# Cross-attention scores as one full-precision matmul, with earlier context and value-weight splits

## The reference

```python
q = (query @ wq).reshape(bs, sq, N_Q_HEADS, D_K).transpose((0, 2, 1, 3))
k = (key @ wk).reshape(bs, sk, N_KV_HEADS, 1, D_K)   # repeated for the 4 query heads of a group
v = (value @ wv).reshape(bs, sk, N_KV_HEADS, 1, D_V)
q = _apply_rope(q, curr_seq_pos)
k = _apply_rope(k, curr_seq_pos)
raw = jnp.einsum('bhqd,bhkd->bhqk', q, k) / scale
attn = jax.nn.softmax(raw + mask, axis=-1)
out = jnp.einsum('bhqk,bhkd->bqhd', attn, v)
```

## Time and profile before

| | |
|---|---|
| time, median of 3 runs | 913.37 us (911.8 to 914.2) |
| the profiled execution | 913.87 us |
| its span, first to last instruction | 911.5 us |
| busy in the span: PE, PEld | 869.6 us (95%), 721.2 us (79%) |
| DVE, ACT, POOL | 654.2 us (72%), 473.1 us (52%), 556.1 us (61%) |
| mean granted clock of TensorE | 0.988 |

### The profile page before, as it was taken

One profiled execution on the slowest core, in us unless ns is written; L12 is line 12 of the kernel. 1 busy time (PEld: TensorE's weight loads), 2 busy tenths in 40 slices (PEclk: granted clock), 3 DMA queues, 4 the chain that ended last, 5 costly groups with the idle time before them and its releaser, 6 DMA issues.

```text
span 911.5 us, 15714 instructions
## 1 busy us (share of the span) xinstructions
PE 869.6 (95%) x4780; PEld 721.2 (79%) x4780; DVE 654.2 (72%) x2171; ACT 473.1 (52%) x1509; POOL 556.1 (61%) x486
## 2 busy tenths in 40 slices
PE   7998899899999799999999999999999998999995
PEld 6787777687777588888888888888888887787884
DVE  5465688778877677777777777777777778546546
ACT  5335777877773355555555555555555556340310
POOL 4625866776677666666666666666666688463002
PEclk9999999999999999999999999999999999999998
DMA  8678999768768011311311313113122123000000
GB/s 284 242 222 190 222 205 177 164 164 171 162 202 300 26 36 38 130 39 36 128 36 45 118 36 127 36 36 128 36 78 85 36 70 105 12 24 24 24 12 35
DMA packets 68370, 96.64 MB, mean 106 GB/s; under 512 B 7232, under 2 KB 44352, under 8 KB 67264
## 3 DMA queue, kind: packets, MB, share of 16 engines
q1 hardware_dynamic: 68288, 95.65, 37.4%
HBM read 68.33 MB, written 27.26 MB: 105 GB/s over the span
## 4 chain that ended last, share of the span: by engine, by line
PE 79%; POOL 6%; DVE 5%; issue 4%; ACT 3%; DMA 1%; SPq 1%; POOLq 0%; ACTq 0%; DVEq 0%
PE banks L35 65%; PE banks L1135 4%; PE banks L1115 3%; PE banks L767 3%; PE banks L785 2%; PE banks L1136 2%; PE banks L758 1%; POOL x L1683 1%; POOL B_wv L171 1%; ACT C_prob L1056 1%; DMA heads_k<-heads_k_d 1%; POOL C_t L1271 1%; POOL B_prob L581 1%; PE banks L122 1%; SPq L213 1%
## 5 line engine op out<-in xcount | busy, mean ns | idle before, releaser
L35 PE MATMUL banks<-C_wo,C_o 128*128 128x512 f32 x768 | 191.8, 399 | 1.9 <-DVE C_o L1232 1.0
L35 PE MATMUL banks<-xT,C_w 128*128 128x512 f32 x768 | 186.6, 392 | 1.1 <-DVE xT L137 0.8
L35 PEld LDWEIGHTS banks<-xT,C_w 128*128 128x128 f32 x768 | 144.3, 189 | 31.9 <-issue 2.0
L35 PEld LDWEIGHTS banks<-C_wo,C_o 128*128 128x128 f32 x768 | 140.5, 190 | 30.6 <-issue 1.9
L1047 ACT ACTIVATE C_q<-C_t 128x512 fp32r<-128x512 f32 x64 | 40.5, 632 | 166.1 <-POOL C_t L1271 166.1
L688 ACT ACTIVATE B_prob<-B_prob,B_top 128x128 f32<-128x128 f32 x256 | 99.5, 391 | 40.1 <-DVE B_top L853 40.0
L1279 POOL TENSOR_TENSOR C_q<-C_t,C_q 128x512 fp32r<-128x512 f32 x64 | 82.8, 1294 | 46.0 <-ACT C_q L1047 46.0
L1056 ACT ACTIVATE C_prob<-C_prob,C_top 128x128 f32<-128x128 f32 x256 | 99.0, 391 | 0.0
L581 POOL TENSOR_TENSOR B_prob<-B_prob,B_rden 128x512 f32<-128x512 f32 x64 | 66.5, 1041 | 36.3 <-DVE B_rden L862 36.2
L1271 POOL TENSOR_TENSOR C_t<-C_t,C_t 128x512 f32<-128x512 f32 x64 | 82.8, 1294 | 6.2 <-DVE C_t L1189 5.9
L171 POOL TENSOR_TENSOR C_w<-stage,C_w 128x512 fp32r<-128x512 f32 x32 | 41.1, 1285 | 54.6 <-ACT C_w L166 54.5
(11 more groups left out here) (147 smaller groups left out, 1918.4 us busy)
## 6 DMA issues: line engine op xcount, KB each, us to landing
C_kv<-cross_kv_d SPq DMA_DIRECT2D x8, 2048.0 KB, 8.5
cross_kv_d<-B_k_out SPq DMA_DIRECT2D x16, 512.0 KB, 3.4
cross_kv_d<-B_v_out SPq DMA_DIRECT2D x16, 512.0 KB, 4.7
stage<-wq_dram SPq DMA_DIRECT2D x32, 256.0 KB, 2.6
stage<-wo_dram SPq DMA_DIRECT2D x32, 256.0 KB, 2.6
heads_q<-heads_q_d SPq DMA_DIRECT2D x96, 64.0 KB, 4.0
heads_k<-heads_k_d SPq DMA_DIRECT2D x96, 64.0 KB, 4.1
heads_q_d<-cT SPq DMA_DIRECT2D x8, 512.0 KB, 2.6
```

Of the source, the lines that this page charges most:

```text
L35: mm = eng.matmul(out, stationary[i], moving[j], start=first and n == 0, stop=last and n == len(PASSES) - 1)
```

## The change

- Cross scores: the rotated keys and queries are kept as plain float32, and scores(n) is one float32 matmul of 128 columns for each head, into bank n % 2; it waits for minima(n - 2). The hi and lo copies of keys and queries go (`key_hi`, `key_lo`, `tile_hi`, `tile_lo`), POOL's sum writes the key or query tile itself, the stored keys take half the bytes, and DVE's L1202 goes. The mask is negated once by ACT.
- Context pieces are loaded behind tiles 7 to 15 and split with tiles 16 to 20.
- The first four value pieces are split ahead of step 0.
- ROW, ROOT and NORMAL stand one step earlier.

```diff
-    PIECES = (("k", 0, -1), ("v", 0, 0), ("v", 1, 0), ("v", 2, 1), ("v", 3, 1), ("o", 0, 3), ("o", 1, 4), ("k", 1, 6),
+    PIECES = (("k", 0, -1), ("v", 0, -1), ("v", 1, -1), ("v", 2, -1), ("v", 3, -1), ("o", 0, 3), ("o", 1, 4), ("k", 1, 6),
-    OT, CLOSE, ROW, ROOT, NORMAL, TURN, TAKE = 13, (14, 15), 16, 17, 18, 19, 20
+    OT, CLOSE, ROW, ROOT, NORMAL, TURN, TAKE = 13, (14, 15), 15, 16, 17, 19, 20
...
+    LOAD_BEHIND = {7: (0,), 9: (1,), 11: (2,), 13: (3, 4), 15: (5, 6, 7)}
+    CONTEXT_AT = (16, 17, 18, 18, 19, 19, 20, 20)
...
-            if i >= self.QK // 2 and i % 2 == 1:
-                self.load_piece(eng, self.CONTEXT + (i - self.QK // 2) // 2)
-        for n in range(self.CONTEXT + C, len(self.pieces)):
-            self.load_piece(eng, n)
+            for n in self.LOAD_BEHIND.get(i, ()):
+                self.load_piece(eng, self.CONTEXT + n)
...
+            wait(eng, self.s_kout[j % 2], 16 * (j // 2))
             t1, t2 = self.t1[j % 2][:, :], self.t2[j % 2][:, :]
-            eng.tensor_tensor(t1, t1, t2, ALU.add).then_inc(self.s_sum, 1)
+            eng.tensor_tensor(self.k_out[j % 2][:, :, :], by_batch(t1), by_batch(t2), ALU.add).then_inc(self.s_sum, 1)
...
+    def negate_mask(self, eng):
+
+        eng.wait_ge(self.s_mask, 16)
+        eng.activation(self.mask[:, :, :], self.mask[:, :, :], ACT.Copy, scale=-1.0).then_inc(self.s_negated, 1)
...
             if n % self.Q == 0:
-                eng.wait_ge(self.s_qlo, n + self.Q)
+                eng.wait_ge(self.s_sum, n + self.Q)
...
-            wait(eng, self.s_top, n)
+            wait(eng, self.s_top, n - 1)
             tok = slice(s % 4 * S, (s % 4 + 1) * S)
-            both = self.kv[g % 2][:, 2 * S * s:2 * S * (s + 1)]
+            keys = self.kv[g % 2][:, S * s:S * (s + 1)].bitcast(F32)
             for h in range(self.Q):
-                out = self.sc[:, h // 2, h % 2, :, :].rearrange("p j s -> p (j s)")
-                q = self.q[s // 4]
-                eng.matmul(out, q[0][:, h, tok], both, start=True, stop=False)
-                mm = eng.matmul(out[:, 0:S], q[1][:, h, tok], both[:, 0:S], start=False, stop=True)
+                mm = eng.matmul(self.sc[n % 2][:, h * S:(h + 1) * S], self.q[s // 4][:, h, tok], keys, start=True, stop=True)
...
-            heads = self.prob[:, n % 2, :].rearrange("p (a h s) -> p a h s", a=2, h=2)
-            for a in range(2):
-                added = eng.tensor_tensor(heads[:, a], self.sc[:, a, :, 1, :],
-                                          self.mask[:, n % B, :].unsqueeze(1).broadcast_to([P, 2, S]), ALU.subtract)
-            added.then_inc(self.s_masked, 1)
-            eng.wait_ge(self.s_masked, n + 1)
             eng.memset(self.carrier[:, :], 0.0)
             for h in range(self.Q):
                 last = eng.tensor_tensor_reduce(
-                    self.prob[:, n % 2, h * S:(h + 1) * S], self.sc[:, h // 2, h % 2, 0, :],
-                    self.prob[:, n % 2, h * S:(h + 1) * S], 1.0, 3.4e38, ALU.add, ALU.min,
-                    self.top[:, n % 2, h:h + 1])
+                    self.prob[:, n % 2, h * S:(h + 1) * S], self.sc[n % 2][:, h * S:(h + 1) * S],
+                    self.mask[:, n % B, :], 1.0, 3.4e38, ALU.add, ALU.min, self.top[:, n % 2, h:h + 1])
```

More of the change, by code:

```diff
@@ L271, in pieces_with @@
         return [self.AHEAD + i] if i < C else [self.VALUES + i - self.Q_DONE] * (0 <= i - self.Q_DONE < C) + \
-            [self.CONTEXT + i - self.QK] * (i >= self.QK)
+            [self.CONTEXT + k for k, tile in enumerate(self.CONTEXT_AT) if tile == i]
     def load_piece(self, eng, n):
@@ L473, in __init__ @@
         self.v_out = pool("v_out", 88, [P, 2, HG, 2, P], F32R)
-        self.k_out = [pool(f"k_out{i}", (96, 132)[i], [P, 4, 2, S], F32R) for i in range(2)]
+        self.k_out = [pool(f"k_out{i}", (96, 132)[i], [P, 4, S]) for i in range(2)]
         self.bout = pool("bout", 126, [P, D])
@@ L542, in sync @@
                 loaded += 1
-            j = self.tile("k", n, 4)
+            j = self.tile("k", n, 2)
             if j is not None:
[L545 to L549, removed]
+                eng.wait_ge(self.s_sum, j + 1)
+                eng.dma_start(self.kv_d[j // 2][:, j % 2 * HALF:(j % 2 + 1) * HALF],
+                              self.k_out[j % 2][:, :, :].rearrange("p b s -> p (b s)")).then_inc(self.s_kout[j % 2], 16)
             j = self.tile("v", n, 2)
@@ L693, in scalar @@
             self.value_hi(eng, j)
-        j = self.tile("k", n, 2)
-        if j is not None:
-            self.key_hi(eng, j)
         self.scalar_pieces(eng, n)
@@ L910, in vector @@
             eng.wait_ge(self.s_pj, self.FILL.index(("k", j)) + 1)
-            wait(eng, self.s_klo, j - 1)
+            wait(eng, self.s_sum, j - 1)
             if j == 1:
@@ L968, in __init__ @@
         self.kv = [pool(f"kv{i}", (36, 16)[i], [P, KV], F32R) for i in range(2)]
-        self.q = [[pool(f"q{half}{lo}", 72 + 16 * half + 8 * lo, [P, self.Q, HALF], F32R) for lo in range(2)]
-                  for half in range(2)]
+        self.q = [pool(f"q{half}", 72 + 8 * half, [P, self.Q, HALF]) for half in range(2)]
         self.prob = pool("prob", 132, [P, 2, D])
@@ L992, in live, with query @@
         return 0 <= n - lag < self.NS
-    def query(self, r, lo):
-        return by_batch(self.q[r // self.Q % 2][lo][:, r % self.Q, :])
+    def query(self, r):
+        return by_batch(self.q[r // self.Q % 2][:, r % self.Q, :])
     def split(self, n):
@@ L1039, in piece_hi @@
         self.ring.hi(eng, self.first + i, self.target(i)[0])
-    def tile_hi(self, eng, r):
-        eng.wait_ge(self.s_sum, r + 1)
-        if r == self.Q:
-            for i in range(2):
-                eng.wait_ge(self.before.s_vout[i], 16 * B)
-        eng.activation(self.query(r, 0), by_batch(self.t1[:, r % 2, :]), ACT.Copy).then_inc(self.s_qhi, 1)
+    def negate_mask(self, eng):
+        eng.wait_ge(self.s_mask, 16)
+        eng.activation(self.mask[:, :, :], self.mask[:, :, :], ACT.Copy, scale=-1.0).then_inc(self.s_negated, 1)
     def exponentials(self, eng, n):
@@ L1185, in rotate @@
         eng.wait_ge(self.s_pj, r + 1)
-        wait(eng, self.s_qlo, r - 1)
+        wait(eng, self.s_sum, r - 1)
         eng.tensor_tensor(by_batch(t1), by_batch(bank), cos, ALU.mult).then_inc(self.s_cos, 1)
@@ L1270, in tile_sum @@
         t1, t2 = self.t1[:, r % 2, :], self.t2[:, r % 2, :]
[L1271 to L1280 removed]
+        eng.tensor_tensor(self.query(r), by_batch(t1), by_batch(t2), ALU.add).then_inc(self.s_sum, 1)
     def gpsimd(self, eng, n):
@@ L1370, in sync @@
             if n == self.DOWN:
-                eng.wait_ge(self.before.s_qlo, self.before.TILES)
+                eng.wait_ge(self.before.s_sum, self.before.TILES)
                 for t, name in ((self.gate, "gate"), (self.gamma, "gamma"), (self.beta, "beta")):
```

56 lines of the change are left out of this document (11 added, 45 removed).

## The result

| | before | after |
|---|---|---|
| median of 4 runs, same chip | 913.79 us (911.8 to 915.87) | 888.68 us (887.6 to 889.99) |
| ratio after / before | | 0.9726, 95% interval 0.9699 to 0.9753 |
| profiled execution, span | 913.87, 911.5 us | 889.44, 887.3 us |
| granted clock over the span | 0.988 | 0.995 |

The account below looks back on a forecast made before the run. It took steady stage C to be bound by PE alone, with PE waits elsewhere; terms -5.4 - 3.1 + 0.5 - 1.1 - 5.5 - 0.9 + 0.6 = -14.9 us gave 898.5 us, range 891 to 907 us.

Parts of the forecast that it names:

- Rows a step forward elsewhere: Stage B, the other six sequences: no such wait to remove, PE's transposes can be slightly late; +0.5 us.
- Steps 0 to 4 of stage C: ACT no longer stalls on query tiles, one division wait and one slow stretch remain; -5.2 us, -5.5 with scores(0).
- More comes back: Rival: remaining idle stretches bring no 1.2 GHz level and score blocks cost the lower bound; 892 to 895 us, 13%.
- Steady steps and end of stage C: Stage C: float32 score blocks cost +0.6 us over 64 steps; removing DVE's L1202 shortens waits at the end, -0.9 us.
- The first rival: Stage C scores dearer, PE's rate set by columns: 1.27 us a block, +20 us, 918 us in all; 8%.
- Start of stage B: Value pieces ready early and heads on time: -3.9 us by step 8, -1.5 for a vanished slow stretch; -5.4 us.
- Steps 32 to 36: Stage B: the root stands ahead of value pieces, the lo half is gone, the fourth value piece is late next; -3.1 us.
- End of stage B: Last division and ACT's copy come earlier without key-tile halves, -1.1 us; scores(0) needs no lo half, -0.3 us.
- After stage C: The rest of the kernel after stage C: no change, 0 us.

Follow-up runs that it names:

- root_first: Kernel before with the row's root ahead of the key tile's lo half in POOL's order, no work removed: 909.37 us, ratio 0.9948.
- pool_load_back: after_rows_back plus one unused 128x512 subtraction on POOL ahead of the root, where the lo half stood: 894.75 us, ratio 0.9789 to the kernel before.
- after_rows_back: Changed kernel with ROW, ROOT and NORMAL put one step later again: 887.65 us, ratio 0.9709 to the kernel before.
- heads_first: Changed kernel with three weight pieces loaded behind the heads of step 12 of stage B instead of ahead: 886.33 us, ratio 0.9719 to the kernel before.
- early_only: Kernel before with only the earlier context loads and splits and the first four value pieces split ahead of step 0: 908.85 us, ratio 0.9946.
- rows_only: Kernel before with only ROW, ROOT and NORMAL one step earlier: 906.49 us, ratio 0.9912.
- scores_only: Changed kernel with the pieces and row steps put back, leaving the full-precision scores and what goes with them: 895.96 us, ratio 0.9798 to the kernel before.
- port_free: Kernel before with POOL made to wait for the row's normalise before its next division: 910.25 us, ratio 0.9971.
- longer_wait: Changed kernel with one more POOL subtraction ahead of the division PE waits for in step 3 of stage C: 890.62 us, ratio 0.9743 to the kernel before.

## Why the prediction was wrong

The sign and most places were right; the size was off by 10 us, and one step failed.

- **Rows a step forward elsewhere, +0.5 us: the failed step.** It said: "In the other six sequences no wait of that kind shows." Five of them had one, 0.86 to 0.95 us each; the row of PE's waits names them in one line, and the timeline of one sequence at steps 32 to 36 was taken for an exception where it was the rule made worse by value pieces. The same step failed a second time in the credits: the 1.27 us of the lo half ahead of the root was counted in steps 32 to 36 only, though POOL's order is the same every eight steps. root_first, pool_load_back and after_rows_back show that this is the cause, and that the row step, which the forecast looked at, adds nothing once the lo half is gone. With the smaller wait at step 46 it makes -2.7 us in each of B 16 to 32 and B 36 to 56, and part of the -2.8 at the end of B: some 7 of the 9.3 us that the forecast's sum lacked. That share is worked out from the waits and the steps of the traces; root_first by itself, with heads and waits moved elsewhere, gave 5 us.
- **Steps 0 to 4 of stage C, -5.2: measured -7.0** from scores(0) to the transposes of step 4, as the forecast counted. The mechanism was right: ACT has no query tile between exponentials, values(1) follows the outputs, one wait for the division is left (2.10 us against my 2.3). The 1.7 us for a slow stretch behind it did not come. That was in part luck: of the five kernels with this same wait of 2.10 us, two (heads_first, pool_load_back) had the stretch, and three had not. The rival "More comes back" named this, the missing stretch at the start of stage B and the cheaper records; all three came, but its 892 to 895 us still lies above 888.68, since it lacked the row waits too.
- **Steady steps and end of stage C, +0.6 - 0.9: measured -1.5.** A record costs 0.112 us and not 0.12. Twenty steps, C 20 to 40, take 149.93 us against 150.40 before, 0.023 a step: 0.023 x 59 = -1.4 us. The -0.9 for the end of C is not there: PE's starts move by 0.2 us from C 59 to 63. The first rival, which scaled the old block of 0.95 us by its columns, would have given +20 us. An estimate says why it fell: if a record streams its 128 columns twice, 8 records want 8 x 256 / 2.4 GHz = 0.85 us, less than the old block's 0.95, which its own 1536 columns (0.64 us) did not fill. What else held the old block up, weight loads as the forecast has it, is argued and not shown.
- **Start of stage B, -5.4: measured -5.4, by two errors that cancel.** At step 8 it was 5.3 us instead of 3.9, because the 1.76 us wait for the division brought no slow stretch. By step 16 the 1.5 us that I had added for the vanished stretch had gone to the heads of step 12. early_only shows the same wait, heads_first that it hangs on the weight pieces loaded ahead of them.
- **Steps 32 to 36, -3.1: measured -3.1.** But early_only and rows_only each get 1.4 to 1.5 us there from a slow stretch that fails to come, and scores_only gets 3.2 alone: it was the missing lo half, with the root's earlier place as a second cover.
- **End of stage B, -1.1 and -0.3: measured -2.8**, of which the row and the step-46 wait of the last sequence are a part. The 0.94 us wait for ACT's copy is gone whole. The row step gives nothing here: the transposes just before wait 0.96 us (257.03) in the changed kernel and 0.30 in after_rows_back, which gains 0.2 us more over the stretch. The rest is not separated further.
- **After stage C, 0: measured +1.0**, a slow stretch behind a wait of 1.25 us that before had too, there without the stretch. after_rows_back has the wait and no stretch (-0.6).

## What to carry over

A wait that recurs with the loop hides from any search for steps that stand out: read the totals of waits per line first, divide by the count, and ask for every removed operation what stands behind it in each round, not only where the trace looks worst. Two edits that cover the same wait don't add (31 us in parts, 24 together): time each part alone and leave it out of the whole. And an edit that speeds up the stretch ahead of a transfer makes the transfer the next thing to be late.

## What the hardware showed

- **A normalise on DVE is held up by a POOL operation that started before it.** L114 (float32, both ends in the on-chip buffer) takes 0.52 to 0.55 us alone, 1.25 us beside a division that began 0.07 us earlier, and 1.48 to 1.51 beside a subtraction that takes the longer 1.26 to 1.29; in each case it ends 0.28 us behind the POOL operation. Where L114 is first (191.09 after), POOL's division takes 1.25 us instead of 1.04. The Trainium skill (SBUF — State Buffer, Who interferes with whom) calls this an exclusive lock on a port pair that VectorE in its two-port mode and GpSimd share, held for the whole instruction, the second one blocked. The traces agree, in both orders, though not to the last tenth: the blocked normalise ends 0.28 us behind the other and not its full 0.52. port_free shows what it costs: 0.7 us of PE's time a sequence.
- **Plain float32 matmuls** with 128 columns of weights and 128 moving columns are two records of 275 ns each, 0.112 us from start to start. The Trainium skill (FP8 and Floating Point Precision, TensorE Precision Notes) has four passes for a true float32 product; 4 x 128 columns in 0.223 us is 2.3 columns a ns, so the trace agrees. Only the four are the skill's; that a reduced product takes one pass, as the prediction has it, is read from rows, 512 columns in 0.227 us. Weight loads start 0.112 us apart too in the new block and 0.115 in the old one, so no run here tells whether columns or weight loads set the pace.
- **The 1.2 GHz level after an idle time is not settled by the length of that time alone.** In the 14 profiled executions PE idled 1.2 to 2.75 us 60 times outside start and end, and a slow stretch came behind 22 of them; behind all six above 2.75 us. The same wait of 1.25 us in the feed-forward stage had one in six kernels and none in eight, and waits of 2.64 us in early_only had none at 180 us and one at 307 us. Of the 24 waits between 1.9 and 2.75 us 13 had one. A forecast should price such a stretch at about half of its 1.4 us (longer_wait) there, and not, as mine did, at all of it.
